# A two-block adapter kernel on one core: the list of adapters in a transfer of its own, six warming products of the preamble's ones, tile 0's first piece in two halves on two queues

## The reference

```python
# block 0: a dense product and a mixture of low-rank experts (E=8, rank 16), top 2 of the router
logits = x @ Wr.T + 5.0 * one_hot(language_id)       # (b, t, 8)
gates  = softmax over the two largest logits, scattered back to 8 columns
h      = einsum('btd,erd->bter', x, A)
x      = x + x @ W.T + 2.0 * einsum('bter,bte,eor->bto', h, gates, B)
# block 1: one of 64 adapters of rank 16 for each batch
x      = x + einsum('bnr,bor->bno', einsum('bni,bri->bnr', x, B1[adapter_id]), A1[adapter_id])
```

## Time and profile before

| what | value |
|---|---|
| median of 3 runs | 95.73 us (95.56 to 96.15) |
| profiled execution | 95.53 us |
| its span | 93.8 us |
| TensorE busy | 89.3 us (95% of the span) |
| VectorE, ScalarE, GpSimd busy | 63.5, 44.3, 36.6 us |

### The profile page before, as it was taken

The page is one execution under the profiler, slowest core; times in us unless marked ns, Lnnn a source line. Parts: engine busy times, 40 slices in busy tenths (PEclk is TensorE's granted clock), DMA queues, the critical chain, the costliest instruction groups (busy, mean ns, idle before and its releaser), DMA issues.

```text
span 93.8 us, 2232 instructions
## 1 busy us (share of the span) xinstructions
PE 89.3 (95%) x757; PEld 73.8 (79%) x757; DVE 63.5 (68%) x219; ACT 44.3 (47%) x89; POOL 36.6 (39%) x44
## 2 busy tenths in 40 slices
PE   4999999999999999999999999999999999999950
PEld 1499888788887888887988888887888898898850
DVE  4357999599694549996592299992530579883980
ACT  2652477352999990398087285960391200001200
POOL 5000867505998500899370019991009000000000
PEclk9999999999999999999999999999999999999999
DMA  1998998973123773943336492322245304141066
GB/s 18 356 330 185 328 400 306 324 251 82 37 89 82 198 246 69 284 171 94 92 68 219 93 369 97 123 64 49 58 151 212 140 0 162 61 183 48 0 233 214
DMA packets 15684, 15.21 MB, mean 162 GB/s; under 512 B 10424, under 2 KB 11704, under 8 KB 15288
## 3 DMA queue, kind: packets, MB, share of 16 engines
q1 hardware_dynamic: 14600, 11.63, 39.6%
q0 software_dynamic: 640, 2.10, 6.6%
q10 hardware_dynamic: 432, 1.33, 4.3%
HBM read 10.81 MB, written 4.24 MB: 160 GB/s over the span
## 4 chain that ended last, share of the span: by engine, by line
PE 92%; DVE 3%; DVEq 0%; issue 0%
PE main L752 16%; PE main L758 15%; PE main L764 15%; PE side L861 5%; PE main L779 4%; PE main L778 4%; PE main L780 4%; PE side L889 3%; PE aw_ps L830 3%; PE aw_ps L828 3%; PE aw_ps L832 3%; PE aw_ps L813 3%; PE main L912 3%; PE side L798 3%; DVE xs L623 3%; PE aw_ps L798 2%
## 5 line engine op out<-in xcount | busy, mean ns | idle before, releaser
L752 PE MATMUL main<-x_hi,w_hi 128*128 128x512 f32 (+1 forms) x64 | 17.4, 393 | 0.0
L758 PE MATMUL main<-x_hi,w_lo 128*128 128x512 f32 (+1 forms) x64 | 16.8, 384 | 0.0
L764 PE MATMUL main<-x_lo,w_hi 128*128 128x512 f32 (+1 forms) x64 | 16.8, 384 | 0.0
L352 POOL TENSOR_TENSOR x_lo<-xs,x_hi 128x512 fp32r<-128x512 f32 x12 | 15.2, 1291 | 0.9 <-DVE aw_lo L504 0.9
L328 POOL TENSOR_TENSOR a_rest<-rows,a_hi 128x512 f32<-128x512 f32 x6 | 7.7, 1300 | 16.1 <-DVE gate_t L559 9.5
L758 PEld LDWEIGHTS main<-x_hi,w_lo 128*128 128x128 f32 x64 | 11.8, 188 | 2.6
L764 PEld LDWEIGHTS main<-x_lo,w_hi 128*128 128x128 f32 x64 | 11.8, 188 | 2.5
L752 PEld LDWEIGHTS main<-x_hi,w_hi 128*128 128x128 f32 x64 | 11.5, 188 | 2.4
L580 DVE TENSOR_TENSOR xs<-main,xs 128x512 f32<-128x512 f32 x15 | 10.0, 685 | 2.9 <-PE main L780 2.8
L451 ACT ACTIVATE down_ops<-down 64x128 fp32r<-64x128 f32 x24 | 7.4, 309 | 7.9 <-DVE down L595 7.5
L425 ACT ACTIVATE a_ops<-a_hi 64x512 fp32r<-64x512 f32 x12 | 7.6, 631 | 7.1 <-POOL a_rest L328 7.0
(11 more groups left out here) (129 smaller groups left out, 146.4 us busy)
## 6 DMA issues: line engine op xcount, KB each, us to landing
out_t<-xs SPq DMA_DIRECT2D x16, 256.0 KB, 2.3
xs<-x_t SPq DMA_DIRECT2D x2, 1024.0 KB, 6.0
b1s<-b_t SPq DMA_DIRECT2D x64, 32.0 KB, 2.0
xs<-x_t SPq DMA_DIRECT2D x4, 256.0 KB, 4.2
ws<-w_t SPq DMA_DIRECT2D x4, 256.0 KB, 4.8
xs<-x_t ACTq DMA_DIRECT2D x1, 1024.0 KB, 8.0
gate_rows<-gate_rows_t SPq DMA_DIRECT2D x3, 256.0 KB
b0s<-b_t SPq DMA_DIRECT2D x1, 256.0 KB, 5.1
```

The source lines that it names most:

```text
L352: nc.gpsimd.tensor_tensor(x_lo[:, t % 2, c], xs[:, t, c], x_hi[:, t % 2, c].bitcast(F32), ALU.subtract).then_inc(x_lo_ready, 1)
L752: nc.tensor.matmul(out_ap, w_hi[:, c, k], x_hi[:, s, k, n], start=(k == 0), stop=False)
L758: nc.tensor.matmul(out_ap, w_lo[:, c, k], x_hi[:, s, k, n], start=False, stop=False)
L764: last = nc.tensor.matmul(out_ap, w_hi[:, c, k], x_lo[:, s, k, n], start=False, stop=False)
```

## The change

There are three edits.

1. The list of 64 adapter ids leaves the id table, which shrinks from 88 to 24 columns, and becomes an input of its own, on one partition. ScalarE issues its transfer, as the last of its four. VectorE wraps and clamps the list in three operations that wait for each other, between the rests of x's pieces 0 and 1; SP waits for VectorE (list_ready) in place of GpSimd. GpSimd's steps have 8 columns.
2. The warming products read a constant of ones that the preamble has written, with a step of 0, in place of the zeros tile; TensorE waits for nothing of VectorE's. The zeros tile shrinks to one column, for ScalarE's first activation.
3. The first piece of tile 0 is issued in two halves of 128 KB: tokens 0 to 255 by SP, as before the first of its queue (x00_loaded), tokens 256 to 511 by ScalarE, between the two transfers of aw. TensorE waits for the first half before its first product and for the second before the third product of quarter 0; ScalarE waits for both before it rounds.

```diff
-        zeros = sb("zeros", [P, 512], BF16)
+        zeros = sb("zeros", [P, 1], BF16)
...
+        list_ids = sb("list_ids", [1, NG * BPG], I32)
...
-        IDS = NG + NG * BPG
+        IDS = NG
...
-            for c in range(K):
+            sp.dma_start(xs[:, 0, 0, 0:GT], x[:, 0, 0, 0:GT]).then_inc(x00_loaded, 16)
+            for c in range(1, K):
                 sp.dma_start(xs[:, 0, c, :], x[:, 0, c, :]).then_inc(x0_loaded[c], 16)
...
-                    clamped[0:1, NG + g * BPG:NG + (g + 1) * BPG], engines=[mybir.EngineType.SP], min_val=0,
+                    list_clamped[0:1, g * BPG:(g + 1) * BPG], engines=[mybir.EngineType.SP], min_val=0,
...
-            sp.wait_ge(clamped_ready, 1)
+            sp.wait_ge(list_ready, 1)
             load_b1(0)
...
             act.dma_start(aws[:, 0], aw[:, 0]).then_inc(aw_loaded[0], 16)
+            act.dma_start(xs[:, 0, 0, GT:], x[:, 0, 0, GT:]).then_inc(x0_loaded[0], 16)
             act.dma_start(aws[:, 1:], aw[:, 1:]).then_inc(aw_loaded[1], 16)
+            act.dma_start(list_ids[:], id_list).then_inc(list_loaded, 16)
...
                 if t == 0:
+                    if c == 0:
+                        act.wait_ge(x00_loaded, 16)
                     act.wait_ge(x0_loaded[c], 16)
...
             x0_rest(0)
+            dve.wait_ge(list_loaded, 16)
+            then_wait(nc.vector.tensor_scalar(list_wrap[:], list_ids[:], 0.0, float(adapters), ALU.is_lt, ALU.mult))
+            then_wait(nc.vector.tensor_tensor(list_wrapped[:], list_wrap[:], list_ids[:], ALU.add))
+            nc.vector.tensor_scalar(list_clamped[:], list_wrapped[:], 0.0, float(adapters - 1), ALU.max,
+                                    ALU.min).then_inc(list_ready, 1)
             x0_rest(1)
...
-                    pe.wait_ge(x0_loaded[k], 16)
+                    if k == 0:
+                        pe.wait_ge(x00_loaded, 16)
+                    else:
+                        pe.wait_ge(x0_loaded[k], 16)
                     for j, h in h_parts():
+                        if k == 0 and j == TILES // 2:
+                            pe.wait_ge(x0_loaded[0], 16)
...
-            pe.wait_ge(zeros_ready, 1)
+            ones = nc.const_aps.tensor(1.0, [P, 512], BF16)
             for _ in range(WARM):
-                nc.tensor.matmul(main[0][:], zeros[:, 0:P], zeros[:], start=True, stop=True)
+                nc.tensor.matmul(main[0][:], ones[:, 0:P], ones, start=True, stop=True)
...
+        "id_list": adapter.reshape(1, B),
         "id_table": np.concatenate([np.repeat(adapter.reshape(-1, P // R).T, R, axis=0),
-                                    np.broadcast_to(adapter.reshape(1, B), (P, B)),
```

More of the change, by code:

```diff
@@ L51, with two_block_kernel @@
 WARM = 6
-def two_block_kernel(nc, x, id_table, w, aw, b0, a1, b1, out, *, tokens_per_batch,
+def two_block_kernel(nc, x, id_list, id_table, w, aw, b0, a1, b1, out, *, tokens_per_batch,
                      experts, rank, adapters):
@@ L138, in two_block_kernel @@
         rank_no = sb("rank_no", [P, 1], I32)
-        IDS = NG + NG * BPG
+        list_ids = sb("list_ids", [1, NG * BPG], I32)
+        list_wrap = sb("list_wrap", [1, NG * BPG], I32)
+        list_wrapped = sb("list_wrapped", [1, NG * BPG], I32)
+        list_clamped = sb("list_clamped", [1, NG * BPG], I32)
+        IDS = NG
         ids = sb("ids", [P, IDS + NB * TILES], I32)
@@ L156, in two_block_kernel @@
         side = [psum(f"side{i}") for i in range(2)]
-        ids_loaded = sem("ids_loaded")
+        ids_loaded, list_loaded = sem("ids_loaded"), sem("list_loaded")
+        list_ready = sem("list_ready")
         x0_loaded = [sem(f"x0_loaded{c}") for c in range(K)]
+        x00_loaded = sem("x00_loaded")
         x_loaded = [None] + [sem(f"x_loaded{t}") for t in range(1, NB)]
@@ L239, in load_b1 @@
                 _, ids = nc.values_load_multi_w_load_instructions(
-                    clamped[0:1, NG + g * BPG:NG + (g + 1) * BPG], engines=[mybir.EngineType.SP], min_val=0,
-                    max_val=adapters - 1, skip_runtime_bounds_check_because="GpSimd clamped them")
+                    list_clamped[0:1, g * BPG:(g + 1) * BPG], engines=[mybir.EngineType.SP], min_val=0,
+                    max_val=adapters - 1, skip_runtime_bounds_check_because="VectorE clamped them")
                 for b, adapter in enumerate(ids):
@@ L338, in _ @@
             pool.wait_ge(clamped_ready, 1)
-            nc.gpsimd.tensor_scalar(row_base[:], clamped[:, 0:NG], float(rank), None, ALU.mult).then_inc(index_step, 1)
+            nc.gpsimd.tensor_scalar(row_base[:], clamped[:], float(rank), None, ALU.mult).then_inc(index_step, 1)
             pool.wait_ge(index_step, 3)
```

## The result

The changed kernel took a median of 96.56 us (96.34 to 97.36, four runs) beside 95.65 for the kernel before (95.25 to 96.15, four runs): a ratio of 1.0101, with a 95% interval from 1.0057 to 1.0146. It is slower by 1%, where I had forecast about 95.5 and a range from 95.0 to 96.0. Its profiled execution took 96.75 us, with a span of 95.0, against 95.53 and 93.8 before.

A forecast was written before the change was run, and what follows sets the result against it. TensorE's queue, with 92% of the span, was taken as the bound. A 0.25 earlier front, less 0.05 for the rest of aw, plus or minus 0.05 for the clock, gave 95.53 - 0.23 = 95.30; median about 95.5, range 95.0 to 96.0 us.

The forecast's parts named there:

- What waits behind the moved issues: Transfers issued later at the front: rest of aw lands at 5.2 to 5.65, wanted at 5.5; cost 0.05 us taken.
- All three signs of being wrong: Wrong if TensorE's quarter 1 passes wait for aw, slow passes are not eight, or VectorE's cast starts after 7.5.
- Warming: TensorE's warming products on the ones start at about 0.95, 0.30 earlier, at no added cost per product.
- First counting product: TensorE's first product that counts starts at 3.72 instead of 3.96 to 3.99: 0.25 us earlier, bounds 0 to 0.35.
- Second half: Tokens 256 to 511 of tile 0's first piece land at 4.2, needed at 4.6: hidden, spare 0.4 us.
- The clock: TensorE's switch from 1.2 to 2.4 GHz: about eight slow passes remain; plus or minus 0.05 us in the sum.
- ScalarE's table load: At ScalarE's front: moves from 1.70 to 2.98 to about 2.55 to 3.85; cost 0, or 0.4 without cover.
- The list: VectorE between x's first and second rests: list lands by 5.8, three steps take 0.6, until 6.4; cost 0.
- the list is late: Rival at VectorE's wait between x's first and second rests: landing at 7.8 costs 1.2, time 96.7 us; chance 0.07.
- The premise: TensorE's queue is full from 1.25 to 87.9, so an earlier front brings the end forward by the same time.
- the ceiling of about 0.5 us: Base products cannot start before W's first block is cast, at 7.92 against 8.45, so at most about 0.5 us gained.
- The first, that the front is held elsewhere: Rival at TensorE's front: halves land together or front held elsewhere; no change, 95.53 to 95.73 us; chance 0.15.

The follow-up runs named there:

- e1: The kernel before with only the warming products changed, to read the constant ones instead of the zeros tile; ratio 0.9984 (0.9953 to 1.0014).
- e2: The kernel before with only the list in its own transfer, third on ScalarE's queue behind all of aw; ratio 1.0006 (0.9979 to 1.0033).
- e4: The changed kernel with ScalarE issuing the rest of aw ahead of the second half; ratio 1.0137 (1.0077 to 1.0197).
- e5: The changed kernel with both halves issued on SP, one behind the other; ratio 0.9997 (0.9957 to 1.0037).
- e7: The changed kernel with tile 0's first piece whole again on SP, list and ones kept; ratio 0.9953 (0.9911 to 0.9994).
- e11: The changed kernel with tile 0's first piece whole again on SP, list and ones kept, measured once more; ratio 0.9987 (0.9967 to 1.0008).
- e3: The kernel before with only tile 0's first piece issued in two halves; ratio 1.007 (1.004 to 1.010).
- e6: The kernel before with only the list moved out, issued by ScalarE between aw's two transfers; median 98.86 us (96.44 to 100.41), no ratio.
- e8: The changed kernel unaltered, run again for a second trace; median 99.49 us (96.26 to 100.52), no ratio.
- e9: The kernel before with ScalarE waiting for VectorE's first pad before issuing the rest of aw, still second; ratio 1.0104 (1.0010 to 1.0199).
- e10: The changed kernel with SP issuing x's third and fourth piece and W only after the first half has landed; ratio 1.0041 (1.0010 to 1.0073).

## Why the prediction was wrong

**The step that failed** is the one headed "What waits behind the moved issues". It put the rest of aw, issued 0.43 later, at 5.65 "if its flight stays, at 5.2 if the amount queued ahead of it sets it", and took 0.05 us. It landed at 6.87; TensorE had been ready at 5.13; the term was 1.79 us. All three signs of being wrong came: passes at quarter 1 wait for aw, four passes are slow and not eight, and VectorE's cast starts at 8.49. Both of my bounds were wrong in kind. I counted what must be moved in total by then, and not what a later issue is up against. SP's four issues of x take 1.85 us from 0.80, so the third piece goes out at about 1.7 and the fourth at 2.2. Issued at 1.22, aw's rest is ahead of them and took 3.1 to 4.0 us in seven traces (before, e1, e2, e4, e5, e7, e11). Issued at 1.70 to 1.88, what ScalarE sends stands against them and took 5.2 to 6.1 in six traces (the changed kernel, e3, e4 with the half, e6, e8, e9), whatever its place, whether it had 204 or 128 KB, whatever stood ahead of it on its own queue. (The list's 256 bytes, issued at 1.70 in e2, were in by 5.17.) With x's third and fourth piece and W held back on SP, the issue at 1.70 took 3.5 (e10).

How the bytes were shared out can be read from windows of the changed kernel (span of the window, busy of PE, PEld, DVE, ACT, POOL with counts, granted clock, share of the DMA engines, GB/s):

```profile
2.00:3.00 1.00, 1.00 (x4) 0.30 (x2) 0.62 (x5) 0.24 (x1) 0.17 (x1) 1.00 0.83 254
3.00:4.00 1.00, 0.98 (x4) 0.46 (x3) 0.00 (x0) 1.00 (x1) 0.00 (x0) 1.00 1.04 340
4.00:5.00 1.00, 1.00 (x8) 0.92 (x7) 0.20 (x1) 0.99 (x4) 0.00 (x0) 1.00 0.86 205
5.00:6.00 1.00, 0.12 (x2) 0.00 (x0) 0.49 (x1) 0.29 (x1) 0.00 (x0) 1.00 1.01 385
6.00:7.00 1.00, 0.08 (x1) 0.09 (x1) 0.45 (x3) 0.00 (x0) 0.00 (x0) 1.00 1.03 393
```

Until 6.87 that makes 254 + 340 + 205 + 385 + 0.87 x 393 = 1526 KB. All of tile 0 and aw together is 1024 + 272 = 1296 KB, so the amount of the front does not explain the landing: part of the 1526 KB is W, while x's third piece was not yet in (ScalarE starts on it at 7.20). In the same five windows ScalarE's queue alone (q10; its 1.46 MB in all are aw, the half, the list and a later megabyte of x) moved (packets, MB, time of its packets as a share of 16 engines):

```profile
q10 hardware_dynamic: 184, 0.12, 42.6%
q10 hardware_dynamic: 92, 0.08, 28.6%
q10 hardware_dynamic: 65, 0.10, 53.1%
q10 hardware_dynamic: 65, 0.08, 22.5%
q10 hardware_dynamic: 8, 0.01, 2.7%
```

ScalarE's queue was thus served all along, and TensorE's wait ends with its last 8 packets of 434, which start after 6.0. The five other late traces end alike: 7 to 17 packets of ScalarE's queue start after 6.0, where in before, e1, e2, e5, e7, e11 and e10 none starts after 5.0. The engines also moved less in total in all six late traces: 205 to 272 GB/s in one of the two microseconds from 4 to 6, where before, e1, e2, e5, e7 and e11 moved 365 to 406 in both. The Trainium skill, "DMA: Bandwidth & Descriptors", section "Queues, rings and completion order", has each DMA engine take turns between the queues that have work. If both queues got the same bytes by turns, which it does not say, ScalarE's 400 KB would be through after some 800 KB, which the windows reach at 5.0; that is an estimate, and the trace is almost 2 us later than it. Why the last packets are so late is not shown by any run here and stays open. Shown is that the later issue brings the delay (e9), and that the delay is gone when x's third and fourth piece and W are held back together (e10); which of these it takes was not tried.

**The sum's other terms.** Warming: forecast at 0.95, measured 0.84, cost of the step-0 operand 0 (e1). First counting product: forecast 3.72, measured 3.58, since the first half and aw's quarter both landed earlier than I took. Second half: forecast at 4.2 and hidden, measured 1.22 + 2.8 = 4.0 and hidden (in e8 it took 3.8, and TensorE waited 0.19 for it). The clock: eight slow passes were forecast, and in this execution the last four of the eight took 0.63 against 1.09 for the first four, so that the first quarter was through 5.95 - 5.13 = 0.8 earlier. About 0.4 of this is the earlier start; the other 0.4 is the clock, which the sum had at plus or minus 0.05. So the start was right and rather too small, and the clock's term was mis-sized, to the fast side; the second quarter was not ready to take up what they gave.

**What I put beside other work.** ScalarE's table load moved by a microsecond and cost nothing, as forecast. x's second piece came early: SP, which waits for it, issues W's second block at 4.64 instead of 5.39. That the third would also be late (7.20 instead of about 6.0) I did not see, and did not cost, because I looked only at the fourth. The list: VectorE's three steps took the 0.6 us forecast but started at 6.48, not 5.8; VectorE was done with the second rest of x at 7.05 + 0.67 = 7.72 and the cast waited until 8.49, for W and not for the list. The rival "the list is late" thus had the direction right, but the landing, before 6.48, stayed under the 6.6 from which it counts a cost; in e2, issued after aw's two transfers alone, the list came in time. W's first block at 8.49 instead of 7.49 was the second thing that I had as unmoved. It hides behind TensorE's own delay here; in e10 it is what ends last.

**The premise** that a front moved by some time moves the end by the same time held: 79.17 us behind the front against 79.19. It held in the wrong direction. No kernel went beyond the ceiling of about 0.5 us: e1, e5, e7 and e11, which lose nothing at the front, bring the base products 0.21 to 0.44 us forward and are at 0.9953 to 0.9997, with intervals that reach, or all but reach, no change. None of the kernels tried beats the one before by a clear margin.

**The rivals.** None named the mechanism. The first, that the front is held elsewhere, was nearest, but I gave it only the transfers that the first product waits for, and a time of no change. The Trainium skill's rule weighed there ("DMA: Bandwidth & Descriptors", section "Issuing engines are not separate DMA queues") did not hold in the form in which I used it: the halves did not land together at 3.8 but at 3.4 and 4.0. What it says, that transfers of all issuing engines run on the same 16 DMA engines and interleave, the trace agrees with: from 4 to 5 us either queue moved 0.10 MB. It gives no price for a later issue.

## What to carry to other kernels

When transfers are issued from several queues, list all issues at the front in one order of time, and ask of each that the change moves what it is now up against; the amount to be moved in total did not tell here who waits. An issue 0.5 to 0.7 us later cost 1.6 to 2.6 at the landing here, beside bulk pieces that another queue issued at the same time. A transfer that the first engine needs second should leave its queue before the bulk of the others, or the bulk should wait for it, and then be checked for who is late in its place.

## What the runs showed that was not expected

An idle stretch at the front can cost more than itself, through TensorE's clock. (It need not: the changed kernel's first trace has the wait of 1.79, and its passes stay at 0.46 for four.) In e4 TensorE had reached the 2.4 GHz level, waited from about 4.5 to 6.96, and was put back to 1.2 GHz while it was busy again; windows of e4, columns as above:

```profile
7.00:7.50 0.50, 0.50 (x4) 0.50 (x5) 0.00 (x0) 0.50 (x1) 0.00 (x0) 1.00 0.97 359
7.50:8.00 0.50, 0.50 (x5) 0.50 (x4) 0.34 (x1) 0.50 (x2) 0.00 (x0) 0.62 0.47 147
8.00:11.00 3.00, 3.00 (x15) 3.00 (x14) 2.90 (x8) 1.72 (x4) 1.48 (x3) 0.50 0.69 208
11.00:12.00 1.00, 1.00 (x11) 1.00 (x10) 0.97 (x4) 0.60 (x1) 0.83 (x3) 0.98 1.16 416
```

The granted clock is 0.50 from 8 to 11 us. In e8, the changed kernel's second trace, the second quarter's passes and those after it still take 0.91 for four, the 1.2 GHz distance, until 13.7 (the granted clock of the windows reads 1.00 there, so the distance has to tell):

```profile
7.87 1.28 PE side L820 x4
9.15 0.91 PE aw_ps L820 x4
10.05 0.91 PE side L820 x4
10.96 0.91 PE aw_ps L820 x4
```

That execution took 100.52 us. The kernels with the wait at the front (e3, e4, e6, e8, e9) took 98 us or more in 17 of 32 runs, the changed kernel itself in three of its eight; e1 and e2 took no more than 96.5 in any of 24. Whether the wait alone makes such executions is not shown: on the chip on which e5, e6, e7 and e8 ran, e5 and e7 took over 97 (98.12 at most) in four of twelve runs each, and the kernel before in two of 23, and no trace of those was taken.
